# Moving an elementwise clamp from VectorE to GpSimd, and result stores from GpSimd's queue to SyncE's, in a deformable-convolution kernel

## The reference

```python
om = conv(x, w_off) + b_off                      # 27 maps: 9 y offsets, 9 x offsets, 9 masks
py = off_y + row + ky;  px = off_x + column + kx  # per pixel and tap
y0, x0 = floor(py), floor(px);  wy, wx = py - y0, px - x0
sampled = v00*(1-wy)*(1-wx) + v01*(1-wy)*wx + v10*wy*(1-wx) + v11*wy*wx
out = einsum('bckhw,ock->bohw', sampled * sigmoid(mask), w) + b
out = relu(batchnorm(out)) + x
```

## Time and profile before

| what | value |
|---|---|
| median of 3 runs | 2105.48 us |
| the profiled execution's own time | 2114.59 us |
| its span, first to last instruction | 2112.8 us |
| PE, DVE, ACT, POOL busy, share of the span | 67%, 74%, 57%, 19% |
| granted TensorE clock over the span | 0.861 |
| sampling stage | from 664 to 1906 us |

### The profile page before, as it was taken

The page is one execution under the profiler, slowest core; times in us unless marked ns, Lnnn a source line. Parts: engine busy times, 40 slices in busy tenths (PEclk is TensorE's granted clock), DMA queues, the critical chain, the costliest instruction groups (busy, mean ns, idle before and its releaser), DMA issues. The chain is left out here.

```text
span 2112.8 us, 59688 instructions
## 1 busy us (share of the span) xinstructions
PE 1425.9 (67%) x24174; PEld 952.9 (45%) x24175; DVE 1554.0 (74%) x1718; ACT 1206.3 (57%) x1755; POOL 394.7 (19%) x743
## 2 busy tenths in 40 slices
PE   4746897000003999999999999899999998991520
PEld 4623332000002666666666666666666666661210
DVE  5326000899613999999999999999999999994115
ACT  1212222655202877887787787787787777780102
POOL 2000000766210121122212211212212211211000
PEclk9769899555555999999999999999999999996565
DMA  3086787699987999999999999999999999951008
GB/s 128 1 182 189 204 235 198 211 341 335 289 239 175 251 257 247 257 249 251 257 246 253 252 253 250 252 247 246 256 251 251 253 254 248 242 147 25 4 1 374
DMA packets 278320, 464.89 MB, mean 220 GB/s; under 512 B 71356, under 2 KB 235027, under 8 KB 274469
## 3 DMA queue, kind: packets, MB, share of 16 engines
q1 hardware_dynamic: 252496, 425.67, 73.7%
q0 software_dynamic: 20528, 21.23, 3.8%
q10 hardware_dynamic: 5030, 14.25, 2.2%
HBM read 354.00 MB, written 106.91 MB: 218 GB/s over the span
## 5 line engine op out<-in xcount | busy, mean ns | idle before, releaser
L937 PE MATMUL ps_even_v<-tent_x,stage 32*128 32x171 f32 (+3 forms) x5568 | 533.3, 319 | 133.6 <-DVE G L1059 107.1
L1013 ACT COPY even_v<-ps_even_v 128x1008 f32<-128x1008 f32 (+2 forms) x464 | 450.8, 972 | 279.7 <-PE ps_odd_v L937 279.7
L1059 DVE TENSOR_TENSOR G<-odd_y,ps_odd_v 128x1008 f32<-128x1008 f32 (+1 forms) x448 | 533.8, 1192 | 66.2 <-PE ps_odd_v L937 55.6
L937 PEld LDWEIGHTS ps_even_v<-tent_x,stage 32*128 32x128 f32 x5568 | 431.6, 185 | 283.8 <-issue 257.3
L1067 DVE TENSOR_TENSOR G<-even_v,ps_even_y 128x1008 f32<-128x1008 f32 (+2 forms) x464 | 538.5, 1161 | 1.8
L937 PE MATMUL ps_odd_v<-tent_x,stage 32*128 32x171 f32 (+3 forms) x5568 | 534.9, 321 | 0.0
L956 PE MATMUL ps_r<-G,conv_w 128*32 128x224 f32 (+3 forms) x9264 | 477.3, 333 | 4.4 <-issue 3.8
L937 PEld LDWEIGHTS ps_odd_v<-tent_x,stage 32*128 32x128 f32 x5568 | 422.7, 185 | 0.5 <-issue 0.5
L920 PE MATMUL ps_odd_y<-rows,sel 32*128 32x504 f32 (+1 forms) x448 | 218.7, 488 | 276.1 <-DMA rows<-scratch_parts 276.1
L868 POOL DMA_DIRECT2D scratch_conv<-res x448 | 216.0, 489 | 927.8 <-ACT res L1020 893.4
L956 PEld LDWEIGHTS ps_r<-G,conv_w 128*32 128x32 f32 x9264 | 263.2, 109 | 162.6 <-issue 110.5
(11 more groups left out here) (158 smaller groups left out, 1044.9 us busy)
## 6 DMA issues: line engine op xcount, KB each, us to landing
place<-scratch_px SPq DMA_DIRECT2D x768, 147.0 KB, 3.5
odd_y<-scratch_full SPq DMA_DIRECT2D x576, 196.0 KB, 5.0
rows<-scratch_parts SPq DMA_DIRECT2D x192, 220.5 KB, 5.0
x<-scratch_xh SPq DMA_DIRECT2D x48, 406.0 KB, 6.3
stage<-scratch_xt SPq DMA_DIRECT2D x192, 96.0 KB, 4.4
scratch_parts<-parts SPq DMA_DIRECT2D x6, 2688.0 KB, 12.9
scratch_om<-om ACTq DMA_DIRECT2D x64, 196.0 KB, 7.3
scratch_full<-tent_y SPq DMA_DIRECT2D x12, 784.0 KB, 9.3
```

The lines of the kernel that those rows point to most:

```text
L937: m = nc.tensor.matmul(sub(ps_v[g % 2], 0, 128, i * 512 + lo + first, dims), stage[32 * g:32 * g + 32, j * IMAGE + v * C:j * IMAGE + (v + ...
L1013: nc.scalar.copy(two(even_v[(STEPS * it + p) % 2], ROW, 2 * p), two(ps_v[0], 512, 2 * p)).then_inc(even_kept, 1)
L1059: nc.vector.tensor_tensor(sub(G, 0, 128, slot(it, v) + lo, [[ROW, 2]] + straight), weights, sub(ps_v[1], 0, 128, lo, [[512, 2]] + straight ...
```

## The change

Three things move; the arithmetic and the number of transfers stay. `cap` goes from VectorE's program to GpSimd's. The four stores of each result block go from GpSimd's queue to SP's, between SP's loads. GpSimd's program is written step by step, so that its copies and signals stand between the caps. The loads of the odd weights were issued tap by tap already and stay so.

```diff
@@ SyncE
+                def store(pair, blk):
+                    sp.wait_ge(res_ready, BLOCKS * pair + blk + 1)
+                    b = blk % 2
+                    for j in range(4):
+                        i, h = j // 2, j % 2
+                        sp.dma_start(dram("conv", (pair * 2 + i) * O * HW + (blk * BLOCK + h * UNIT_ROWS) * W,
+                                            [[HW, O], [1, UPX]]), res[b][32 * j:32 * j + O, :]).then_inc(res_stored[b], 16)
...
+                        if at := block_of(it, p):
+                            if at[2] == BLOCK // 2 - 1:
+                                store(at[0], at[1])
                 unrolled(PAIRS, body)
+                store(PAIRS - 1, BLOCKS - 1)
+                for b in range(2):
+                    sp.wait_ge(res_stored[b], 64 * results(PAIRS, b)[1])
@@ GpSimd
-                def store(pair, blk):
-                    pool.wait_ge(res_ready, BLOCKS * pair + blk + 1)
...
+                def cap(it, p):
+                    n = STEPS * it + p
+                    pool.wait_ge(distant, n + 1)
+                    wait(pool, sampled, n - 1)
+                    lo, hi = both(p)
+                    nc.gpsimd.tensor_scalar(tent_x[(STEPS * it + p) % 2][:, lo:hi], dist_x[(STEPS * it + p) % 2][:, lo:hi], 1.0, 1.0,
+                                            ALU.min, ALU.subtract).then_inc(tent_ready, 1)
+                cap(0, 0)
+                cap(0, 1)
 
                 def body(it, last):
...
+                    for p in range(STEPS):
+                        if p == 0:
...
+                        if to := ahead(it, p + 2, last):
+                            cap(*to)
+                        if p == GROUP - 2:
+                            pool.wait_ge(distant, STEPS * it + GROUP)
+                            pool.wait_ge(place_loaded[2], it + 1)
+                            pool.tensor_tensor(turn[:, 2:3], turn[:, 4:5], turn[:, 4:5], ALU.add).then_inc(place_read, 1)
+                        if p == GROUP:
+                            pool.wait_ge(even_spread, STEPS * it + GROUP)
+                            pool.wait_ge(rows_loaded[2], it + 1)
+                            pool.tensor_tensor(turn[:, 3:4], turn[:, 4:5], turn[:, 4:5], ALU.add).then_inc(rows_read, 1)
@@ VectorE
-                def cap(it, p):
-                    n = STEPS * it + p
-                    dve.wait_ge(distant, n + 1)
-                    wait(dve, sampled, n - 1)
...
-                        if to := ahead(it, p + 2, last):
-                            cap(*to)
```

More of the change, by code:

```diff
@@ L871, in body @@
-                def body(it, last):
[L872 to L891, removed]
@@ new lines, in cap @@
+                def cap(it, p):
[7 more added lines that the diff above has]
+                cap(0, 1)
+                def body(it, last):
+                    for p in range(STEPS):
+                        if p == 0:
+                            wait(pool, distant, STEPS * it)
+                            pool.wait_ge(place_loaded[0], 16 * PER_PLACE * (2 * it + 1))
+                            pool.tensor_tensor(turn[:, 0:1], turn[:, 4:5], turn[:, 4:5], ALU.add)
+                            pool.tensor_copy(sub(place[2], 0, 128, 0, [[W, KK], [1, W]]),
+                                             sub(place[0], 0, 128, 0, [[GROUP * W, KK], [1, W]])).then_inc(place_loaded[2], 1)
+                            wait(pool, even_spread, STEPS * it)
+                            pool.wait_ge(rows_loaded[0], 16 * PER_ROWS * (2 * it + 1))
+                            pool.tensor_tensor(turn[:, 1:2], turn[:, 4:5], turn[:, 4:5], ALU.add)
+                            pool.tensor_copy(sub(rows[2], 0, 128, 0, [[W, KK], [1, W]]),
+                                             sub(rows[0], 0, 128, 0, [[GROUP * W, KK], [1, W]]).bitcast(fp32)).then_inc(rows_loaded[2], 1)
+                        if to := ahead(it, p + 2, last):
[8 more added lines that the diff above has]
+                            pool.tensor_tensor(turn[:, 3:4], turn[:, 4:5], turn[:, 4:5], ALU.add).then_inc(rows_read, 1)
@@ L892, in _ @@
                 unrolled(PAIRS, body)
-                store(PAIRS - 1, BLOCKS - 1)
-                for b in range(2):
-                    pool.wait_ge(res_stored[b], 64 * results(PAIRS, b)[1])
             @block.tensor
```

## The result

The changed kernel takes 2227.56 us (median of 4 runs, 2224.04 to 2229.38), the kernel before in the same job 2106.32 us. The ratio is 1.057, with a 95% interval of 1.055 to 1.059. The direction of the forecast was right and its size was not: 121 us slower where 68 were forecast, and 2227.56 lies above the range's end of 2208.

The account below looks back on a forecast made before the run. VectorE narrowly bounds the kernel before; afterwards SP would, at 69.5 + 12.5 = 82.0 us a pair, 4.6 over 77.4. Over 15 pair lengths that is +69, the rest gains 1.5: 2174 us, range 2112 to 2208.

Parts of the forecast that it names:

- SP becomes the bound: Sampling stage: SP's issues, with stores added, set 82.0 us a pair instead of 77.4; chance 0.65, 2150 to 2195 us.
- the waits of weight_odd for odd_y at a batch's head: VectorE, sampling stage: DMA waits ending on odd_y ahead of weight_odd, once in seven steps, 1 to 2 us each.
- rival 4: GpSimd's cap blocks VectorE at SBUF: 82.4 us a pair, near 2175 us; chance 0.03 together with a cap over 1.8 us.
- Rivals 1, 2 and 3: SP keeps up, 2081 us, 0.13; long issues shrink by half, 2120 us, 0.11; SP keeps idle time, 2210 us, 0.08.
- 12.5 us a pair: SP in the sampling stage: 28 stores a pair, priced at 1.78 us for a block's four with the gap behind.
- to cost the same afterwards, also to a store: SP's long issues at instruction fetches: 10.9 fetches and 7.3 us a pair, expected unchanged by the change.
- The 0.67 us: Cost to SP of one instruction fetch, taken as 7.3 us of long issues over 10.9 fetches a pair.
- 82.0: Forecast pair length in us in the sampling stage: SP's 69.5 plus 12.5 for stores, with no idle time added.
- a pair of seven blocks gains 1.5 us: Cap off VectorE: four steps go from 10.68 to 10.47 us, so a pair could run in 75.9 us.
- 2.57 us for the PSUM loop: Step limit through the one PSUM buffer once the cap leaves VectorE: 1.25 + 1.20 + 0.12 us, against 2.64.
- hidden up to about 1.8 us: Cap on GpSimd: 1.95 us of room before the sample using it, so a cap of 0.6 to 1.2 us costs nothing.
- The granted clock is 1.00, so no gain or loss hides in the clock: Sampling stage of the kernel before, 14 pairs: the clock was read as full, so no time was assigned to it.

Follow-up runs that it names:

- the two-tap kernel: The changed kernel with TensorE's reduction cut to two of its nine taps, SP's program the same: 2201.35 us, ratio 1.0442.
- the last two rows of the table: Kernels with stores on ScalarE, one a step: cap on GpSimd with distance ahead of keep_odd, 2107.83 us; cap on VectorE, without that reordering, 2107.78 us.
- the first experiment: The changed kernel with the cap back on VectorE and the stores left on SP: 2219.34 us, ratio 1.0545 to the kernel before.
- the next kernel: The changed kernel with stores on ScalarE, one a step instead of four at once, and GpSimd's two signals one step earlier: 2116.19 us, ratio 1.0036.

## Why the prediction was right in direction and short in size

**Right: SP becomes the bound.** SP's idle time went from 7.9 to 1.5 us a pair by its waits, a pair is as long as SP's issues (65.2 loads + 14.4 stores + 6.1 gaps + 0.4 idle = 86.1 us, by rounded terms, against 86.03), and doubling the stores took the loss from 8.6 to 22.2 us a pair. Right as well: the waits of weight_odd for odd_y at a batch's head, 35 of them at 2.9 us on average, up to 5.9, and not 1 to 2; no contention with GpSimd (weight_odd at most 1206 ns, as in the earlier trace rows, so nothing speaks for rival 4); four undisturbed stores in 1.81 us. Rivals 1, 2 and 3 are out: the long issues stayed, and SP kept almost no idle time.

**The step that failed: "12.5 us a pair" for the stores on SP, beside 7.3 us for the fetches, which were "to cost the same afterwards, also to a store".** It priced a store as one without a fetch at it, and left the long issues at their old 7.3 us. The mechanism held; this term of the sum was too small. Measured are 14.4 us of issue time (28 x 0.511) and 1.4 us more of gaps, less 0.4 of loads: 15.4 us, 2.9 over the forecast. At the stores' median, 28 x 0.421 = 11.8 us, so 2.6 us of the store time are long issues. Most of that is explained by the traces: while SP still waited one tenth of the time, it let 27 of 152 fetches pass without a long issue, 20 of them in its waits; when it is never idle, only 4 of 151 pass. The 0.67 us was an average over both kinds of fetch. One that meets a busy SP costs 0.9 us by the long issues, and about 1.1 by the two-tap kernel. My text had named this as the thing that could make it wrong, and had given it no price.

**Two smaller terms.** SP's load before was 70.3 us a pair by the gaps, and 69.5 by the table of waits: 0.8. An idle rest of 0.4 remained. With the 2.9 these account, within rounding, for the 4.0 us by which 86.0 exceeds 82.0. Over 15 pair lengths that is 60 us; by medians the miss is 54, since the stage lost 129 us and the medians only 121. That difference lies outside the mechanism and made the miss look smaller.

**The gain of the step was nothing.** "a pair of seven blocks gains 1.5 us" rested on 2.57 us for the PSUM loop; it is 2.64 to 2.67. The term was small, and hidden behind SP in the changed kernel, so it did not cause the miss. It matters for what the change could ever bring: on its own the cap's move is worth 0 us (the last two rows of the table), or a loss of 8 us if ScalarE's order stays.

**The cap's price was wrong and cost nothing.** 1.89 us, where 0.6 to 1.2 were taken; even the "hidden up to about 1.8 us" was passed. The copy was no near row for an operation with constants. Since SP's 86 us leave a step 0.3 us more than it needs, the first experiment saw none of it. With SP free it costs 8 us in one order of ScalarE's work, and none in another.

**The clock.** "The granted clock is 1.00, so no gain or loss hides in the clock" was true of the kernel before alone; after the change it is 0.96. Since SP's issues fill the pair, none of the miss needs it.

**Left open.** How a fetch holds up SP's issue is not shown; what is shown is that long issues stand at fetches and that fewer fetches make SP faster. Likewise it is shown that TensorE stands until a fetch has come, and not why large transfers delay the fetch. Why four stores at once on ScalarE cost 81.25 us a pair was not taken apart: the store placement and the late signals both changed in the next kernel.

## What to carry to other kernels

Count the queue that issues the loads as an engine of its own: add its issues and gaps at their medians, add one long issue for every instruction fetch (also for those that its idle time still hides), and put the sum against its idle time before giving it anything more. An engine whose bars touch is not thereby the bound; look for a loop of the same length through a buffer beside it, and open that first. A work-around for a queue's load (fewer, larger transfers) has to be measured for what it does to everyone who shares the DMA engines, instruction fetches included.

## What the runs showed of the hardware

- An arithmetic instruction with two constants on GpSimd takes 1893 ns for 128x504 f32 and one with one constant 1464 ns, while a copy takes 594. VectorE takes 417 for the two-constant one.
- A DMA issue on SP costs 0.42 us for 16 or 32 rows and 0.59 to 0.60 for 48 or 128 rows, by the medians, and 0.49 to 0.53 on average for 16 rows when SP is never idle. The Trainium skill's page "DMA: Bandwidth & Descriptors", section "Issuing engines are not separate DMA queues", calls such time usually small relative to the DMA itself. For the single store the trace agrees (0.42 us against 2.8 us until it lands); for the kernel it does not follow, as 28 issues a pair on a queue that had 7.9 us to spare cost 121 us of 2106.
- An instruction fetch costs a busy SP 0.9 us (its long issues) to 1.1 us (the two-tap kernel). `place` in transfers of three times the size costs the kernel before 9.9%; for a good part of it TensorE waits, up to 4.5 us at a time, until a fetch has come.
